# FFN, second attention and experts of a gated cross-attention program in one program block with SBUF placed by hand

## Chip, cores and metric
One core of a Trainium2 chip. The metric is the device time of one execution in microseconds (us); lower is better.

## What is computed
Two gated cross-attention layers over x (32 x 112 x 256) and a context (32 x 375 x 256), 16 heads of 16, each followed by a feed-forward part: first a three-layer one with weights of +1 and -1, then eight experts of which each token uses one.

```python
x = x + tanh(g_xattn[0]) * L0_xattn(layernorm(x), ctx, ctx, mask_ik, ...)
x = x + tanh(g_ffn[0])   * L0_ffn(layernorm(x), k0, k1, k2, s0, s1, s2)     # 256 -> 1024 -> 1024 -> 256
x = x + tanh(g_xattn[1]) * L1_xattn(layernorm(x), ctx, ctx, mask_if, ...)
x = x + tanh(g_ffn[1])   * L1_ffn(layernorm(x), Wr, W1, W2)
# L1_ffn: eidx = argmax(softmax(x @ Wr)); rank of a token in its expert, kept below cap = 448;
#         xe = x[dispatch]; ye = relu(xe @ W1[e]) @ W2[e]; y[dispatch] += ye * probability
```

## The kernel before
Five stages run one after the other: setup, first attention, FFN, second attention, experts. Each is a program block of its own in which the five engines (PE the matrix engine, ACT, DVE, POOL and SP, which issues most transfers) each run a program written out by hand and wait on each other's semaphores. At the end of a block all engines meet, and then a small block follows in which SP clears the stage's semaphores one by one (`Semaphores.clear`, L93 to L98).

**Attention** (`attention_phase`) is a pipeline over the 32 examples of the batch. In step s, context s is split into a high and a low half-precision part, keys of s-1 are made, values and the row maxima of s-3, exponentials and weighting of s-4, output of s-5; in the second attention examples s-6 to s-16 are normalised, routed to experts and their rows sent to the DRAM buffer `expert_in` (L743). The order of the work inside a step is written out for each engine (`body`). Ahead of the steady part, `run_quads` (L487) interleaves nine steps of `Queries` (L287), which load four examples of x (L326), take statistics (L377), normalise them to `xn` (L364), transpose (L431), multiply by the query weights (L422) and store the result split in two to DRAM (L332), with the first steps of the attention, by the lists ORDER (PE, ACT, DVE, POOL) and LOADS (SP), L481 to L484. The DVE program of the second attention begins with memsets of padding (L1198 to L1219). `store_max` (L643) writes the row maxima, turned, into row 96 of `q_stack`; the next score product of PE waits for it. POOL multiplies eight of twelve units of the probabilities by a mask (L724), and in the second attention it carries much of the routing (L729 to L781).

**Blank rows.** `clear_experts` (L676) fills `expert_in` (3612 KB) with rows that belong to nobody, from SP's queue at step 8 of the first attention.

**FFN** (`ffn_phase`) works on groups of four examples. Step s does the sixteen hidden products of group s-1 (z 0 to 15, L1627) and its output (L1638), and beside them normalises group s: statistics at z 9 (L1477), xn at z 11, transposes on PE at z 12, the low part at z 13. `run_steps` (L68) writes out the first four steps and the last one; steps 4 to 7 run in a hardware loop. SP loads x (L1447) and mask_in (L1448) of a group as soon as the output of the group two before is done, and stores the cut mask for the second attention (L1451, L1453). POOL stores the output y (L1466), which the second attention reads. The FFN's weights `ffn_w` are given free after the FFN.

**Experts** (`experts_phase`): per expert SP loads w1 and w2 (L1717, L1718) and the expert's 448 rows (L1720); ACT and DVE split eight pieces of the weights into high (L1802) and low (L1842) halves, beside the products of the expert before; PE transposes the rows (L1758) and multiplies by w1 (L1775) and w2 (L1789); POOL gathers the rows of the output so far (L1738) and scatters the sums (L1743). For the first expert nothing runs beside the splitting. DVE begins with memsets of `x_old` (L1837).

```python
        setup_phase(nc, m, a)
        attention_phase(nc, m, 0, a["x"], x1, ...)
        ffn_phase(nc, m, a, x1, x2, a["mask_BxSxS2_if1"], add_1, keep_1)
        of_ffn.close()
        attention_phase(nc, m, 1, x2, out, ...)
        experts_phase(nc, m, a, expert_in, out)
```

Of the kernel before, what the change touches and what calls it, by code (L numbers as in the profile page):

```python
# [1 line left out]

# [13 lines left out]
P = 128  # L16
# [27 lines left out]
LARGEST = 3.0e38  # L44

# [54 lines left out]

def flamingo_program(nc, a, out):
# [10 lines left out]
    with ExitStack() as ctx:  # L112
        def sb(name, shape, dt):
# [23 lines left out]
        of_ffn = ctx.enter_context(ExitStack())  # L137
        m["ffn_w"] = [of_ffn.enter_context(nc.sbuf_tensor(f"ffn_w{n}", shape, F16))
                      for n, shape in enumerate(((P, KC, F), (P, FC, F), (P, FC, D)))]
        setup_phase(nc, m, a)  # L140
        attention_phase(nc, m, 0, a["x"], x1, a["ctx_1024"], (m["mask_add"], m["keep"]), q_split,
                        a["mask_1x1xSxS2_ik1"], (None, expert_in))
        ffn_phase(nc, m, a, x1, x2, a["mask_BxSxS2_if1"], add_1, keep_1)
        of_ffn.close()
        attention_phase(nc, m, 1, x2, out, a["ctx_1024"], (add_1, keep_1), q_split, None,
                        (a["L1_ffn_Wr"], expert_in))
        experts_phase(nc, m, a, expert_in, out)


# [137 lines left out]
class Queries:  # L287


    def __init__(self, m, layer, x_in, mask, q_split, sb, sem):  # L290
        self.m, self.layer, self.mask = m, layer, mask
# [195 lines left out]
def run_quads(count, lag, eng, order, queries, body):  # L487
# [7 lines left out]
    for s in range(1 + max(s for what, s in order if what == "a"), count + lag):  # L495
        body(Quad(s // 4, s % 4))


def attention_phase(nc, m, layer, x_in, x_out, context, masks, q_split, mask_in, routing):
# [3 lines left out]
    with ExitStack() as ctx:  # L503
        sems = Semaphores(nc, ctx)
        def sb(name, shape, dt):
            return ctx.enter_context(nc.sbuf_tensor(name + tag, shape, dt))

        def sem(name):
            return sems.new(name + tag)

        def many(count, make, name, *args):
            return [make(f"{name}{n}", *args) for n in range(count)]

        SPILL = P - CK
        WIDE = CH * P
        ctx_in = many(2, sb, "ctx_in", [P, KC, S2], F32)
        ctx_high = many(4, sb, "ctx_high", [P, KC * S2 + SPILL], F16)
        ctx_low = many(4, sb, "ctx_low", [P, KC * S2 + SPILL], F16)
        k_high, k_low = many(2, sb, "k_high", [P, KC, WIDE], F16), many(2, sb, "k_low", [P, KC, WIDE], F16)
        k_stack = many(4, sb, "k_stack", [P, NP * WIDE], F16)  # L520
        q_stack = many(4, sb, "q_stack", [P, NP * 2 * S + P - S], F16)
        values = many(2, sb, "values", [CK, CH, H, QUAD], F32)
        masked_scores = sb("masked_scores", [S, 3, S2], BF16)
        row_max = sb("row_max", [S, H], F32)
        max_parts = sb("max_parts", [S, 2, P], F16)
        max_t = many(2, sb, "max_t", [H // 2, S], F16)
        probs = sb("probs", [CK, UNITS, GT], F32)
        heads_t = sb("heads_t", [P, GT], F32)
        inverse = sb("inverse", [S, H], F32)
        heads_q = sb("heads_q", [S, H, DK], F32)  # L530
        if layer:
            heads_n = sb("heads_n", [P, KC, S], F32)
        else:
            heads_high, heads_low = sb("heads_high", [P, KC, S], F16), sb("heads_low", [P, KC, S], F16)
            wo_high, wo_low = sb("wo_high", [P, KC, D], F16), sb("wo_low", [P, KC, D], F16)
        x_sum = many(4, sb, "x_sum", [S, D], F32)
        router, expert_in = routing
        if layer:
            wr = sb("wr", [P, KC, E], F32)
            stats, mean_var = sb("stats", [S, 6], F32), sb("mean_var", [S, 2], F32)  # L540
            root, shift, half, spread = (sb(n, [S, 1], F32) for n in ("root", "shift", "half", "spread"))
            sent_rows = sb("sent_rows", [S, 3 * G, ROW], F32)
            xt = many(2, sb, "xt", [P, KC, S], F32)
            before_f, before = sb("before_f", [S, S], F32), sb("before", [S, S], BF16)
            ones = sb("ones", [S, S], BF16)
            number, logits = sb("number", [S, G, E], F32), many(2, sb, "logits", [S, G, E], F32)
            shifted, hit, marked, power = (sb(n, [S, G, E], F32) for n in ("shifted", "hit", "marked", "power"))
            chosen, ranks, picked = sb("chosen", [S, G, E], BF16), sb("ranks", [S, G, E], F32), sb("picked", [S, G, E], F32)
            counted, carried = sb("counted", [S, E], F32), sb("carried", [S, E], BF16)
            top, first, chance, rank, over, place = (sb(n, [S, G], F32) for n in  # L550
                                                     ("top", "first", "chance", "rank", "over", "place"))
            put = many(3, sb, "put", [S, G], U32)
            mask_add = many(4, sb, "mask_add", [S, S2 + SPILL], BF16)
            keep = many(4, sb, "keep", [CK, CH, S], I32)
        else:
            mask_add, keep = [masks[0]] * 4, [masks[1]] * 4

        ctx_loaded, q_loaded, k_loaded = many(2, sem, "ctx_loaded"), many(2, sem, "q_loaded"), many(2, sem, "k_loaded")
        max_loaded = [many(2, sem, f"max_loaded_{half}_") for half in range(2)]
        masks_loaded = many(4, sem, "masks_loaded")  # L560
        x_loaded, x_stored = many(4, sem, "x_loaded"), many(4, sem, "x_stored")
        if layer:
            wr_loaded, measured, rooted, xn_ready = sem("wr_loaded"), sem("measured"), sem("rooted"), sem("xn_ready")
            routes_made, routes_kept, powered = sem("routes_made"), sem("routes_kept"), sem("powered")
            reduced, combined = sem("reduced"), sem("combined")
            before_made, numbered, sent = sem("before_made"), sem("numbered"), many(3 * G, sem, "sent")
        queries = Queries(m, layer, x_in, mask_in, q_split, sb, sem)
        pads_set, ones_set = sem("pads_set"), sem("ones_set")
        ctx_high_ready, ctx_low_ready = sem("ctx_high_ready"), sem("ctx_low_ready")
        k_made, k_high_ready, k_low_ready = sem("k_made"), sem("k_high_ready"), sem("k_low_ready")  # L570
        v_made, v_ready = sem("v_made"), sem("v_ready")
        rows_scored, rows_maxed = sem("rows_scored"), sem("rows_maxed")
        parts_ready, max_turned, max_ready = sem("parts_ready"), sem("max_turned"), sem("max_ready")
        scored, exped, masked, weighted = sem("scored"), sem("exped"), sem("masked"), sem("weighted")
        heads_ready, heads_turned, inverted, normed = (sem("heads_ready"), sem("heads_turned"), sem("inverted"),
                                                       sem("normed"))
        turned_back, back_high_ready, back_ready = sem("turned_back"), sem("back_high_ready"), sem("back_ready")
        wo_split = sem("wo_split")
        projected, summed = sem("projected"), sem("summed")
        ended = ExitStack()  # L580
        block = ended.enter_context(nc.Block())

        row_bank = m["bank"][0:3]
        score_bank = m["bank"][3:6]
        head_bank = m["bank"][6]
        work_bank = m["bank"][7]
        HALF = UNITS // 2
        HH = H // 2
# [17 lines left out]
        def bank_of(n, what):  # L606

            return row_bank[use_of[n.value, what] % 3]
# [1316 lines left out]
```

## Time and profile before

| | us |
|---|---|
| median of 3 runs | 1663.68 (1658.14 to 1667.85) |
| the profiled execution, its own time | 1670.54 |
| its span | 1668.9 |
| PE busy | 1486.5 (89%) |
| DVE, POOL, ACT busy | 1067.6, 853.8, 818.5 |
| mean granted TensorE clock | 0.955 of full speed |
| first PE work of the second attention / last PE work of the FFN | 902.27 / 883.57 |
| first PE work of the experts / last of the second attention | 1489.22 / 1455.44 |

The page divides the span into forty slices; in those at the start of a stage PE's share drops to 4 or less of ten, in all others of the two attentions and the FFN it is 8 or 9. A matrix product's end is modelled, so that "busy" at PE only says that nothing was waited for. "x8" at the end of a row of the timeline means that eight like instructions are merged, and the bracket is the idle time of the engine ahead of the row and what ended it.

### The profile page before, as it was taken

Reading aid. Unit: us, or ns where it says so; the run is one execution under the profiler, and the core shown is the slowest. Engines: PE = TensorE matmul, PEld = TensorE weight load, DVE = VectorE, ACT = ScalarE, POOL = GpSimd, SP = SyncE. Lnnn points to the kernel's source line nnn. Section 1 sums busy time; section 2 is a strip of 40 time slices with the busy share of each in tenths; the row PEclk is TensorE's granted clock in tenths of the full one; section 3 lists DMA queues with packets and bytes.
Section 4 is the critical chain, followed back from the end, with each engine's and each line's share of the span. In section 5 each row is a group of like instructions: output and inputs, shape, how many; then the busy total and the mean of one; then the engine's idle time right before and its main releaser. Section 6 shows DMA issues by size and latency. Waiting matters only on the chain. (4 is left out here: it accounts for less than half of the span.)

```text
span 1668.9 us, 41243 instructions
## 1 busy us (share of the span) xinstructions
PE 1486.5 (89%) x15435; PEld 1082.2 (65%) x15435; DVE 1067.6 (64%) x3580; ACT 818.5 (49%) x1907; POOL 853.8 (51%) x904
## 2 busy tenths in 40 slices
PE   0889899999999499999994789999999999529997
PEld 0457678777777266666663457777777777417776
DVE  5767677777777255555545677777777777226663
ACT  3456566666666222222221456666667666314442
POOL 0077677777777000000000177778888888723442
PEclk9999899999999699999997999999999999759999
DMA  5755544544441222222214866655566553063440
GB/s 147 197 130 147 124 102 104 101 102 102 101 93 39 61 63 63 63 71 63 62 36 117 203 125 115 116 113 110 113 128 122 121 108 57 21 187 101 155 137 19
DMA packets 214248, 172.67 MB, mean 103 GB/s; under 512 B 69930, under 2 KB 207599, under 8 KB 214056
## 3 DMA queue, kind: packets, MB, share of 16 engines
q1 hardware_dynamic: 208424, 160.34, 41.8%
q0 software_dynamic: 5632, 9.78, 1.9%
q8 instruction: 119, 1.95, 0.5%
q14 instruction: 73, 0.60, 0.1%
HBM read 95.86 MB, written 41.15 MB: 82 GB/s over the span
## 5 line engine op out<-in xcount | busy, mean ns | idle before, releaser
L1100 ACT ACTIVATE probs_a<-bank 125x448 f32<-125x448 f32 x768 | 384.7, 540 | 23.7 <-PE bank L944 15.0
L724 POOL TENSOR_TENSOR probs_a<-probs_a,mask_keep 125x448 int32<-125x448 int32 x256 | 285.5, 1138 | 108.2 <-ACT probs_a L1100 108.1
L1272 DVE CUSTOM_DVE_ANT_0 masked_scores_a<-bank,mask_add_a 112x375 bf16<-112x375 f32 x512 | 262.5, 547 | 106.0 <-PE bank L914 105.5
L724 POOL TENSOR_TENSOR probs_a<-probs_a,keep_a 125x448 int32<-125x448 int32 x256 | 286.1, 1137 | 66.4 <-ACT probs_a L1100 65.0
L1272 DVE CUSTOM_DVE_ANT_0 masked_scores_a<-bank,mask_add 112x375 bf16<-112x375 f32 x512 | 261.1, 550 | 85.5 <-PE bank L914 82.0
L914 PE MATMUL bank<-k_stack_a,q_stack_a 96*128 96x375 f16 x1024 | 292.4, 326 | 5.8 <-DVE row_max_a L1272 4.6
L944 PE MATMUL bank<-q_stack_a,k_stack_a 97*128 97x224 f16 x1536 | 254.6, 261 | 11.7 <-DMA q_stack_a<-max_t_a 10.7
L944 PEld LDWEIGHTS bank<-q_stack_a,k_stack_a 97*128 97x128 f16 x1536 | 147.0, 99 | 72.7 <-DMA q_stack_a<-max_t_a 12.3
L789 POOL TENSOR_TENSOR ctx_low_a<-ctx_in_a,ctx_high_a 128x375 f16<-128x375 f32 x128 | 113.1, 904 | 146.2 <-ACT ctx_high_a L1078 146.1
L1627 PE MATMUL bank<-h0h_f,ffn_w 128*128 128x448 f16 x512 | 180.5, 352 | 0.0
L1627 PE MATMUL bank<-h0l_f,ffn_w 128*128 128x448 f16 x512 | 180.4, 352 | 0.0
L1466 POOL DMA_DIRECT2D x_after_ffn<-y_f x8 | 5.9, 741 | 333.7 <-DVE y_f L1513 333.7
L962 PE MATMUL bank<-probs_a,values_a 125*32 125x112 f32 x6144 | 161.5, 260 | 1.9 <-POOL probs_a L724 1.9
L962 PEld LDWEIGHTS bank<-probs_a,values_a 125*32 125x32 f32 x6144 | 144.8, 110 | 22.6 <-issue 19.5
L1153 ACT ACTIVATE heads_t_a<-bank 128x448 f32<-128x448 f32 x64 | 34.8, 544 | 216.7 <-PE bank L962 216.7
L914 PEld LDWEIGHTS bank<-k_stack_a,q_stack_a 96*128 96x128 f16 x1024 | 99.5, 98 | 45.2 <-DVE row_max_a L1272 13.7
L1578 ACT ACTIVATE h1h_f<-bank 128x448 f16<-128x448 f32 x64 | 34.8, 544 | 152.9 <-PE bank L1627 152.9
L871 PE MATMUL bank<-wv_high,ctx_high_a 128*128 128x256 f16 x384 | 105.3, 274 | 1.4 <-DVE k_low_a L1315 1.4
L871 PE MATMUL bank<-wv_high,ctx_low_a 128*128 128x256 f16 x384 | 104.9, 273 | 0.0
L871 PE MATMUL bank<-wv_low,ctx_high_a 128*128 128x256 f16 x384 | 104.7, 273 | 0.0
L1506 DVE SCALAR_TENSOR_TENSOR h1l_f<-bank,h1h_f 128x448 f16<-128x448 f32 x64 | 39.8, 621 | 97.3 <-ACT h1h_f L1578 97.3
L850 PE MATMUL bank<-ctx_high_a,wk_high 128*128 128x375 f16 x256 | 84.2, 329 | 6.9 <-DVE k_low_a L1315 6.6
(215 smaller groups left out, 3193.0 us busy)
## 6 DMA issues: line engine op xcount, KB each, us to landing
k_stack_a<-k_high_a SPq DMA_DIRECT2D x256, 96.0 KB, 4.0
ctx_in_a<-in_ctx_dram SPq DMA_DIRECT2D x64, 375.0 KB, 3.6
w_in_e<-in_L_ffn_W_dram SPq DMA_DIRECT2D x16, 1024.0 KB, 8.6
k_stack_a<-k_low_a SPq DMA_DIRECT2D x128, 96.0 KB, 4.5
q_stack_a<-q_split SPq DMA_DIRECT2D x128, 84.0 KB, 3.4
q_split<-high_a SPq DMA_DIRECT2D x32, 224.0 KB, 3.7
mask_in_f<-in_mask_BxSxS_if_dram SPq DMA_DIRECT2D x8, 656.2 KB, 6.4
mask_keep<-keep_f SPq DMA_DIRECT2D x8, 656.2 KB
```

What stands on the lines that cost most here:

```text
L724: pool.tensor_tensor(bits, bits, cols, ALU.mult).then_inc(masked, 1)
L789: pool.tensor_tensor(ctx_low[s.four][:, cols], ctx_in[s.two][:, c, :], ctx_high[s.four][:, cols], ALU.subtract).then_inc(ctx_low_ready, 1)
L850: last = pe.matmul(work_bank[:, 0:S2], w[:, c, j * P:(j + 1) * P], part[p.four][:, c * S2:(c + 1) * S2], start=c == 0 and n == 0, stop=c = ...
L871: last = pe.matmul(work_bank[:, (k % 2) * D:(k % 2 + 1) * D], part[x.four][:, at:at + P], w[:, c, :], start=c == 0 and n == 0, stop=c == K ...
L914: pe.matmul(bank_of(x, h)[:, 0:S2], q_stack[x.four][0:STACK, at:at + P], k_stack[x.four][0:STACK, (h // 2) * WIDE:(h // 2) * WIDE + S2], s ...
L944: last = pe.matmul(bank[:, half * 2 * S:(half + 1) * 2 * S], k_stack[d.four][0:ROWS, at:at + P], q_stack[d.four][0:ROWS, (2 * t + half) * ...
L962: last = pe.matmul(head_bank[QUAD * j:QUAD * (j + 1), t * S:(t + 1) * S], values[d.two][:, k, 4 * t + j, :], probs[:, i, j * S:(j + 1) * S ...
L1100: act.activation(probs[:, i, :], score_bank[i % 3][0:CK, 0:GT], ACT.Exp, scale=DK ** -0.5).then_inc(exped, 1)
L1153: act.activation(heads_t[:, :], head_bank[:, 0:GT], ACT.Copy).then_inc(heads_ready, 1)
L1272: dve.tensor_tensor_reduce(masked_scores[:, use_of[x.value, h] % 3, :], bank_of(x, h)[0:S, 0:S2], mask_add[x.four][:, 0:S2], 1.0, -LARGEST ...
L1506: dve.scalar_tensor_tensor(out=low[:, j, :], in0=z_bank[z % 4][:, 0:GT], scalar=0.0, in1=high[:, j, :], op0=ALU.max, op1=ALU.subtract).the ...
L1627: last = pe.matmul(z_bank[z % 4][:, 0:GT], w[layer][:, c, j * P:(j + 1) * P], part[:, c, :], start=c == 0 and n == 0, stop=c == chunks - 1 ...
```

## The change
FFN, second attention and experts become programs that are run one after the other in one block (`run_block`); there is no meeting of the engines and no clearing of semaphores between them, and all their semaphores are cleared after the experts. Buffers of the three are placed by hand in regions (`Region`), so that the second attention's context, key and query buffers lie outside the FFN's and the first expert's weights and rows outside what the attention still uses. In the last FFN step each engine does the first items of the second attention's ORDER and LOADS (q 0, q 1, a 0). The FFN's steps are all written out. `clear_experts` moves from step 8 of the first attention to step 2 of the FFN. The first expert's weights are loaded in eight pieces in steps 20 to 27 of the second attention and split in steps 28 to 31. The FFN uses the PSUM banks in another order. Where the block end ordered things, there are waits now.

```diff
-        attention_phase(nc, m, 0, ...); ffn_phase(...); of_ffn.close(); attention_phase(nc, m, 1, ...); experts_phase(...)
+        with ExitStack() as first:
+            run_block(nc, attention_phase(m, place, place, sems.new, 0, a["x"], x1, ...))
+            sems.clear()
+        with ExitStack() as second:
+            of_ffn = Region(nc, start, FFN_SIZE)
+            of_start = Region(nc, start + FFN_SIZE, EARLY_SIZE)
+            after = Region(nc, base, start + FFN_SIZE - base)
+            early = Region(nc, start + FFN_SIZE, CTX_SIZE)
+            asked = Region(nc, start + FFN_SIZE + CTX_SIZE, EARLY_SIZE - CTX_SIZE)
+            spare = Region(nc, start + FFN_SIZE + EARLY_SIZE, SPARE_SIZE)
+            last = Region(nc, base, start + FFN_SIZE - base)
...
+            of_the_ffn = Program(*(partial(part, after=attention) for part in ffn[0:5]))
+            run_block(nc, of_the_ffn, attention, experts)
+            sems.clear()

 class Queries:                                       # sync, tensor
+            if self.layer:
+                sp.wait_ge(self.ffn.stored[s % 2], 16 * (s // 2 + 1))
             sp.dma_start(self.xg[s % 2][:, :, :], self.x_rows[s]).then_inc(self.x_loaded[s % 2], 16)
...
+            if self.layer and q == 0:
+                pe.wait_ge(self.ffn.y_ready, G * NG)
...
+            if self.layer and p == 0:
+                pe.wait_ge(self.ffn.kept, 2 * NG)

 def attention_phase(...):
+    def load_beside(sp, s):
+        if layer and 20 <= s < 28:
+            experts.load_first(sp, s - 20)
+    def high_beside(act, s):
+        if layer and 28 <= s < 32:
+            experts.high_first(act, 2 * (s - 28))
+            experts.high_first(act, 2 * (s - 28) + 1)
+    def low_beside(dve, s):
+        if layer and 28 <= s < 32:
+            experts.low_first(dve, 2 * (s - 28))
+            experts.low_first(dve, 2 * (s - 28) + 1)
...                                                   # SP, layer 1
-                if not layer and s.value == 8:
-                    clear_experts()
+        if opening:
+            load_context(Quad(0, 0))
+            body(Quad(0, 0))
+            return
+            sp.wait_ge(ffn.y_ready, G * NG)
+            for n in range(2):
+                sp.wait_ge(ffn.stored[n], 16 * NG // 2)
             sp.dma_start(wr[:, :, :], ...)
-            run_quads(B, LAG, sp, LOADS, queries.sync, body)
+        run_quads(3, B + LAG, sp, LOADS[done:], queries.sync, body, load_beside)
...                                                   # DVE, layer 1, ahead of the memsets
+            for n in range(2):
+                dve.wait_ge(ffn.stored[n], 16 * NG // 2)
+                dve.wait_ge(ffn.add_stored[n], 16 * NG // 2)
+                dve.wait_ge(ffn.keep_stored[n], 16 * NG // 2)

 def ffn_phase(...):                                  # s == NG is the last step
-    z_bank, y_bank, turn_bank = m["bank"][0:4], m["bank"][4:6], m["bank"][6:8]
+    z_bank, y_bank, turn_bank = m["bank"][2:6], m["bank"][6:8], m["bank"][0:2]
-            run_steps(sp, NG, 1, body)
+        for s in range(NG + 1):
+            if s == NG:
+                after.queries.sync(sp, 0)
+                after.queries.sync(sp, 1)
+                after.sync(sp, opening=True)
+            if s == 2:
+                clear_experts()
+            body(Step(s // 2, s % 2))
+            if s == NG:
+                after.gpsimd(pool, opening=True)
+                if s.value == NG and z == 11:
+                    after.queries.vector(dve, 0)
+                if s.value == NG and z == 13:
+                    after.queries.vector(dve, 1)
+                if s.value == NG and z == 12:
+                    after.queries.scalar(act, 0)
+        after.scalar(act, opening=True)
+        after.queries.scalar(act, 1)
+                    if s.value == NG and b == 1:
+                        after.queries.tensor(pe, 1)

 def experts_phase(...):
+    def load_first(sp, n):
+        rows = piece(w1_rows[0], w2_rows[0], n)
+        sp.dma_start(piece(w1_in[0], w2_in[0], n), rows).then_inc(first_loaded, 16)
+    def high_first(act, n):
+        act.wait_ge(first_loaded, 16 * PIECES)
+        act.activation(piece(w1[0][0], w2[0][0], n), ...).then_inc(w_high_ready, 1)
+    def low_first(dve, n):
+        dve.wait_ge(w_high_ready, n + 1)
+        dve.scalar_tensor_tensor(out=piece(w1[1][0], w2[1][0], n), ...).then_inc(w_low_ready, 1)
+                if s.value > 0:
                     sp.dma_start(w1_in[s.slot][:, :, :], ...)
                     sp.dma_start(w2_in[s.slot][:, :, :], ...)
+                else:
+                    for n in range(3 * G):
+                        sp.wait_ge(sent[n], 16 * len(range(n, B, 3 * G)))
                     sp.dma_start(xg[s.slot][:, :, :], ...)
```

## Rows read from the trace of the kernel before

**Rows 1.** Windows, one steady step of the second attention: busy time by engine, clock, DMA.
```profile
1324.70:1339.25 14.55, 14.55 (x191) 11.34 (x190) 10.78 (x44) 9.89 (x25) 13.11 (x16) 1.00 0.62 119
```

**Rows 2.** Chain of waits, its start: start us, us, what.
```profile
1487.82 4.90 DVE w_low_e L1842 x8
...
1493.93 11.61 PE bank L1775 x48
```

**Rows 3.** Timelines by engine, seam from FFN to second attention: start us, us, instruction.
```profile
885.02 0.71 POOL L1466 DMA_DIRECT2D x_after_ffn<-y_f  x1 [37.10 <-DVE y_f L1513]
...
891.81 0.16 DVE L1198 MEMSET max_parts_a<- 112x120 uint32 x1 [7.45 <-PEq L94]
...
896.08 0.16 DVE L1219 MEMSET number_a<- 112x4 f32 x8
...
900.84 1.38 DVE L364 TENSOR_SCALAR xn_a<-xg_a,mean_var_q_a,scale_a 112x256 f32<-112x256 f32 x4
...
902.27 1.76 PE L431 MATMUL bank<-ident,xn_a 112*128 112x112 f32 x8 [18.43 <-DVE xn_a L364]
...
909.54 0.93 PE L431 MATMUL bank<-ident,xn_a 112*128 112x112 f32 x8
...
914.89 0.98 PE L431 MATMUL bank<-ident,xn_a 112*128 112x112 f32 x8 [0.40 <-DVE xn_a L364]
```

**Rows 4.** Timelines of SP and PE, first expert's rows; landing times of all eight such loads.
```profile
1478.36 0.57 SPq L1720 DMA_DIRECT2D xg_e<-expert_in  x1
...
1489.22 1.75 PE L1758 MATMUL bank<-ident,xg_e 112*128 112x112 f32 x8 [33.52 <-DMA xg_e<-expert_in]
...
DMA to landing us min/median/max: 2.0/2.5/16.4
```

**Rows 5.** ACT's heads in three steps of the first attention, PE's wait, the clear's landing.
```profile
160.37 0.54 ACT L1153 ACTIVATE heads_t_a<-bank 128x448 f32<-128x448 f32 x1 [3.28 <-PE bank L962]
...
183.78 0.54 ACT L1153 ACTIVATE heads_t_a<-bank 128x448 f32<-128x448 f32 x1 [3.28 <-PE bank L962]
...
197.40 0.54 ACT L1153 ACTIVATE heads_t_a<-bank 128x448 f32<-128x448 f32 x1 [3.28 <-PE bank L962]
...
172.89 0.93 PE L944 MATMUL bank<-q_stack_a,k_stack_a 97*128 97x224 f16 x4 [7.24 <-DMA q_stack_a<-max_t_a]
...
DMA to landing us min/median/max: 14.3/14.3/14.3
```

**Rows 6.** Timelines of SP, DVE and POOL inside the FFN.
```profile
608.09 0.29 SPq L1453 DMA_DIRECT2D mask_keep<-keep_f  x1
...
628.06 1.40 DVE L1477 BATCH_NORM_STATS2 stats_f<-xg_f 112x6 f32<-112x256 f32 x4
...
691.55 0.71 POOL L1466 DMA_DIRECT2D x_after_ffn<-y_f  x1 [37.94 <-DVE y_f L1513]
730.61 0.71 POOL L1466 DMA_DIRECT2D x_after_ffn<-y_f  x1 [38.35 <-DVE y_f L1513]
```

**Rows 7.** Instructions by source line: last waits seen, semaphore clears (ns, first and last start).
```profile
L1470 POOLq EVENT_SEMAPHORE  x1: 17/17/17, 888.7 to 888.7; - x1
...
L98 SPq EVENT_SEMAPHORE_RANGE_CLEAR  x28: 25/28/30, 889.9 to 891.4; - x28
...
L1381 POOLq COMPARE_BRANCH  x1: 45/45/45, 1468.0 to 1468.0; - x1
...
L98 SPq EVENT_SEMAPHORE_RANGE_CLEAR  x91: 25/30/49, 1471.4 to 1477.1; - x91
```

**Rows 8.** Timelines of SP, ACT and DVE between two steps of the second attention.
```profile
1249.17 0.33 SPq L704 DMA_DIRECT2D out_dram<-x_sum_a  x1
1252.37 0.68 SPq L643 DMA_DIRECT2D q_stack_a<-max_t_a  x1
...
1339.25 0.55 ACT L1153 ACTIVATE heads_t_a<-bank 128x448 f32<-128x448 f32 x1 [3.49 <-PE bank L962]
...
1339.73 0.55 DVE L1272 CUSTOM_DVE_ANT_0 masked_scores_a<-bank,mask_add_a 112x375 bf16<-112x375 f32 x1 [1.36 <-PE bank L914]
```

More of the change, by code:

```diff
@@ L1 @@
+import math
+from collections import namedtuple
 from contextlib import ExitStack
+from functools import partial
 import concourse.bass as bass
@@ L143, in flamingo_program, with place @@
[L143 to L147, printed above, removed]
+        with ExitStack() as first:
+            sems = Semaphores(nc, first)
+            def place(name, shape, dt):
+                return first.enter_context(nc.sbuf_tensor(name, shape, dt))
+            run_block(nc, attention_phase(m, place, place, sems.new, 0, a["x"], x1, a["ctx_1024"],
+                                          (m["mask_add"], m["keep"]), q_split, a["mask_1x1xSxS2_ik1"]))
+            sems.clear()
@@ new lines, in flamingo_program @@
+        with ExitStack() as second:
+            sems = Semaphores(nc, second)
+            start = -(-nc.sbuf_base // 32) * 32
+            of_ffn = Region(nc, start, FFN_SIZE)
[5 more added lines that the diff above has]
+            last = Region(nc, base, start + FFN_SIZE - base)
+            ffn = ffn_phase(m, of_ffn, sems.new, a, x1, x2, a["mask_BxSxS2_if1"], add_1, keep_1, expert_in)
+            sent = [sems.new(f"sent{n}") for n in range(3 * G)]
+            experts = experts_phase(m, last, early, asked, spare, sems.new, a, expert_in, out, sent)
+            attention = attention_phase(m, after, of_start, sems.new, 1, x2, out, a["ctx_1024"], (add_1, keep_1), q_split,
+                                        None, (a["L1_ffn_Wr"], expert_in, sent), ffn, experts)
+            of_the_ffn = Program(*(partial(part, after=attention) for part in ffn[0:5]))
+            run_block(nc, of_the_ffn, attention, experts)
+            sems.clear()
@@ L484, with run_quads @@
          ("a", 2), ("q", 9), ("q", 10))
-def run_quads(count, lag, eng, order, queries, body):
+def run_quads(first, count, eng, order, queries, body, beside=None):
     for what, s in order:
@@ new lines, in turn_maxima, with score_unit @@
+        def turn_maxima(n, half):
+            pe.wait_ge(parts_ready, 2 * n.value + half + 1)
+            wait_bank(pe, n, HALVES[half])
+            dst = bank_of(n, HALVES[half])[:, :].bitcast(F16)[:, 0:S]
+            pe.transpose(dst, max_parts[:, half, :], ident_h[0:S, 0:S]).then_inc(max_turned, 1)
+        def score_unit(d, i):
+            t, k = divmod(i, CH)
+            if i % HALF == 0:
+                pe.wait_ge(max_loaded[i // HALF][d.two], 16 * (d.use2 + 1))
+            if i == 0 and layer:
+                pe.wait_ge(masks_loaded[d.four], 32 * (d.use4 + 1))
+            if i == 0 and isinstance(d.value, int) and d.value == 0:
+                pe.wait_ge(ones_set, 6)
+                pe.wait_ge(queries.low_ready, KC * NG)
+            wait(pe, exped, UNITS * d.value + i - 2)
+            bank = score_bank[i % 3]
+            by_scores = i not in pool_units
+            if by_scores:
+                pe.matmul(bank[:, 0:GT], mask_add[d.four][:, k * CK:k * CK + P],
+                          ident_b[0:S, 0:S].unsqueeze(1).to_broadcast([S, 4, S]), start=True, stop=True)
+            for half in range(2):
+                at = (2 * t + half) * WIDE + k * CK
+                last = pe.matmul(bank[:, half * 2 * S:(half + 1) * 2 * S], k_stack[d.four][0:ROWS, at:at + P],
+                                 q_stack[d.four][0:ROWS, (2 * t + half) * 2 * S:(2 * t + half + 1) * 2 * S],
+                                 start=not by_scores, stop=True, skip_group_check=True)
+            last.then_inc(scored, 1)
```

2327 lines of the change are left out of this document (1163 added, 1164 removed).

## The prediction
> **What bounds the kernel now.** I read the page first: the matrix engine (PE) is busy for 89% of the span, and the slices in which it is not lie at the start of each stage. Then the windows by stretch, for what sets the pace inside a stage: one step of the second attention is 14.55 us and PE is busy for all of it, with POOL at 13.11 and DVE at 10.78 [rows 1]. Then the chain of waits, which runs back from the end over PE alone until it reaches the first expert's first product at 1493.93 and, ahead of that, the splitting of that expert's weights [rows 2]. So inside the stages PE is the limit and a faster helper engine is worth nothing; what can be won lies where PE stands still. The timelines show three such places, and the change touches all three. (1) FFN to second attention: PE waits 18.43 us [rows 3]. (2) Attention to experts: PE waits 33.5 us [rows 4]. (3) Step 8 of the first attention takes 23.41 us, from 160.37 to 183.78, where its neighbour takes 13.62, because PE waits 7.24 us for a small transfer and then runs some time at half clock [rows 5].
>
> **The blank rows (clear_experts).** The 3.6 MB write is issued on SP's queue in step 8 of the first attention and lands after 14.3 us; the transfer of the row maxima that PE waits for is queued behind it [rows 5]. Taken away, the step should be like its neighbour: 23.41 - 13.62 = 9.8 us gained. In the FFN it is issued right behind the keep store of 608.09, so at its old duration it lands near 623. Behind it in the queue lies the load of group 2, which is normalised at 628.06 [rows 6]; that leaves some 5 us for 448 KB. I cost it at nothing. The cover is that the FFN keeps a whole group (38.6 us) of loads ahead; were the cover gone, the price is at most the 9.8 of before. Ends: 0 to -9.8, nearest to 0.
>
> **The FFN without its loop.** Steps 4 to 7 of the FFN ran in a hardware loop. POOL's wait from store to store is 37.94 in an unrolled step and 38.35 in the first looped one [rows 6]; the three other looped ones lie between. With some 0.25 for each of four: 1.0 us gained. Ends: 0 and 1.6.
>
> **First seam.** Before: the last store of the FFN is issued at 885.02 and seen as landed at 888.7 [rows 3, 7]. Then come the end of the block and 28 semaphore clears to 891.4 [rows 7], DVE's memsets from 891.81 to 896.24, loads, statistics, xn of group 0 at 900.84, PE's first transposes at 902.27, the second ones at 909.54, the third at 914.89 [rows 3]. After: loads, statistics, xn and transposes of group 0, and the statistics of group 1, lie inside the last FFN step, in the place where DVE and ACT otherwise prepare a next group that no longer exists, and the two loads and two context loads are issued some 40 us ahead. Only the eight transposes come on PE's path: 0.93 us at full clock [rows 3], so the last store is seen at 889.6. SP and DVE both wait for that store. SP's queue behind this wait holds the router weights and the load of group 2; DVE's holds the memsets and everything after. The memsets take their 4.4 us to 894.0, the reciprocals and xn of group 1 1.8 us (as 0.4 and 1.38 before 902.27 [rows 3]), so the second transposes start near 895.9 instead of 909.54: 13.6 us. In the meantime PE computes the query product of group 0 and then stands still for some 7 us. After the 18 us pause the granted clock was at its lower level, 1.2 GHz (the page's slices), and the eight transposes took 1.76 instead of 0.93 [rows 3]; I expect the lower level here too, so from the second transposes to the third it takes the 7.27 us of the cold pair of before, not the 5.35 of the next: -1.9. That leaves 11.7; I take 11.5. Ends: 3, if the later loads of the prologue, and not this start, set its length, and 13.6.
>
> **Second seam.** Before: POOL has seen all rows sent at 1468.0; the block's end and 91 clears follow to 1477.2 [rows 4, 7]; the rows of expert 0 are loaded at 1478.36 behind 2 MB of weights, and PE starts its transposes at 1489.22 [rows 4]; ACT and DVE split eight weight pieces until 1492.7, and the first product starts at 1493.93 [rows 2]. After: the weights are there and split; SP issues the load of the rows as soon as the last row has landed, at about 1468.1. Its landing took 2.0 us at best and 10.9 in this seam [rows 4]; now it is first in its queue with 2 MB right behind it, so I take 4.0: 1472.1. Transposes (1.75 [rows 4]), one copy and one subtraction: 3.4 us, where it was 4.7 with ACT still on the weights. First product at 1475.5 instead of 1493.93: 18.4 us. Ends: 11.5 and 20. The second expert's weights are asked for some 9 us earlier too, and the next pair at once, since the pieces of expert 0 count as done; both lie in the queue behind what PE waits for first.
>
> **What is given back.** The clears do not vanish, they gather behind the last store: 28 of the FFN and 91 of the attention [rows 7], 1.5 + 5.7 = 7.2 us, on the path that sets the end. Ends: 6.6 and 7.8.
>
> **What the attention takes in.** Steps 20 to 27 each issue one 256 KB piece on SP, between the store at 1249.17 and the maxima of 1252.37, a gap of 3.2 us [rows 8]; at the clear's rate (3.6 MB in 14.3 us) a piece is 1.0 us, so it fits. Steps 28 to 31 each put two pieces on ACT and DVE ahead of the body. ACT stands idle there for 3.49 us, DVE for 1.36 [rows 8]; two low pieces on DVE are 2 x 0.61 = 1.2 us (4.90 for eight [rows 2]). It just fits on DVE, and what is late next is the row maximum and the bank behind it. I take -1.0 in all. Ends: 0 and -12 (the first rival).
>
> **Sum.** 9.8 + 1.0 + 11.5 + 18.4 - 7.2 - 1.0 = 32.5 us. The profiled execution took 1670.54, so one like it would take 1638.0; it was 6.9 us over the median, and against the median of 1663.68 the forecast is 1631 us.
>
> **Rivals.** (A) The attention pays for what it takes in. Each low piece reads two SBUF tiles on DVE while POOL, 13.11 of 14.55 us busy in 16 instructions [rows 1], masks the probabilities; if each piece waited for one POOL instruction of 0.82 us, that is 6.6 us, and 2 MB of loads at the clear's price (9.8 us for 3.6 MB) are 5.4. Against it: the seam between two steps, where the pieces lie, is the one place where POOL has only small work. 12 instead of 1.0 lost: 1642. The Trainium skill, "SBUF — State Buffer", section "SBUF: two separate sides", has the rule: DVE instructions with two SBUF inputs and GpSimd instructions that read SBUF share one port pair, and the loser blocks for the whole instruction. By that rule the 6.6 us would stand and the sum would be 5.6 us smaller; in the trace of before DVE split weights only while POOL computed nothing, so no row there decides it. (B) The prologue's gain is not kept, because its loads and the traffic through the split queries set its length: 3 instead of 11.5, 1640. For it: the queue of SP is long there. Against it: each later load waits on xn, which comes earlier. (C) The clear keeps its price in the FFN: group 2 is late, DVE waits in order, PE's transposes after it: 1641. Against it: the 5 us of room. (D) Slower: the new placing makes the second attention's own step longer. PE has no slack there, POOL 1.4 us. The gain of 32.5 is eaten at 1.0 us in each of 32 steps, and from 1.3 us on the kernel is slower than before, 1672 or more. For POOL's eight masks that would be (1.4 + 1.3) / 8 = 0.34 us each on 0.82. Nothing in the rows points to it. (E) The change does not do what it says: the waits that stand in for the two block ends come as late as these, both seams give nothing, the clears still come on top, and 9.8 + 1.0 - 7.2 - 1.0 = 2.6 are left: 1661.
>
> **How the numbers follow.** Forecast 0.68, A 0.11, B 0.09, C 0.07, D 0.03, E 0.02. Half a per cent, 8.3 us, is about what a measurement of this kernel can tell from no change. Forecast, A, B and C lie below 1655 and make faster 0.95; E is same, 0.02; D slower, 0.03. The range: the unknown ends of the forecast's terms reach from 38 (13.6 at the first seam, 20 at the second, no loss in the attention) to some 22 gained, and A to C lie at 1640 to 1642; with the runs' own spread of 5 us, 1622 to 1643.
>
> **What would show it.** Right: step 8 of the first attention 13.6 long; FFN steps of 38.6 with PE full; the second transposes of attention 1 some 11 us after the last store is issued and the clock low again for some 10 us; steps 20 to 31 at 14.55 to 14.81; the first product of expert 0 some 7 us after the last row is seen landed; 139 or more clears at the end, over 8 us. Wrong: a step of 28 to 31 above 15, PE idle in FFN step 2 behind a transpose, or a wait for the first rows of over 6 us.

## The result and the profile after

The changed kernel takes 1650.72 us, the median of 8 executions (1646.99 to 1659.43); the kernel before takes 1665.75 in its 8 beside them. The ratio of the two is 0.9919 (95% interval 0.9897 to 0.9942): faster beyond the interval, but by less than one per cent, 15.0 us where 32.5 were forecast. 1650.7 lies outside the range of 1622 to 1643. The profiled execution took 1659.43 (span 1657.2); it is the longest of the eight, as will matter below.

Where the gains were forecast they are there. Timelines of the changed kernel, the first attention and the first seam:

```profile
156.95 0.54 ACT L1255 ACTIVATE heads_t_a<-bank 128x448 f32<-128x448 f32 x1 [3.28 <-PE bank L1065]
170.58 0.54 ACT L1255 ACTIVATE heads_t_a<-bank 128x448 f32<-128x448 f32 x1 [3.28 <-PE bank L1065]
...
875.39 0.71 POOL L1582 DMA_DIRECT2D x_after_ffn<-y_f  x1 [6.05 <-DVE y_f L1631]
885.64 1.75 PE L512 MATMUL bank<-ident,xn_a 112*128 112x112 f32 x8 [7.46 <-DVE xn_a L439]
893.62 0.93 PE L512 MATMUL bank<-ident,xn_a 112*128 112x112 f32 x8
902.62 0.99 PE L512 MATMUL bank<-ident,xn_a 112*128 112x112 f32 x8 [0.38 <-DVE xn_a L439]
```

The step that held the blanking write is 13.63 long (170.58 - 156.95), where it was 23.41 [rows 5]: 9.8 gained. The transposes of group 0 now lie inside the FFN, so these three are the second, third and fourth of the stage. The second come 10.25 after the last FFN store (24.52 before [rows 3]), the third 18.23 (29.87 before). Counted from that store to the first heads copied by ACT (965.48, before 987.16), the seam is 12.05 shorter, where 11.5 was forecast. The forecast had the eight transposes of group 0 in it, and they lie ahead of the store: the last FFN step is 38.72 instead of 37.82, so like for like the seam gained 11.15. The second seam:

```profile
1464.59 0.32 SPq L1875 DMA_DIRECT2D xg_e<-expert_in  x1
...
1468.29 1.75 PE L1911 MATMUL bank<-ident,xg_e 112*128 112x112 f32 x8 [15.82 <-DMA xg_e<-expert_in]
...
1471.43 0.53 PE L1928 MATMUL bank<-x_high_e,w_high_e 128*128 128x448 f16 x1 [1.38 <-DVE x_low_e L2004]
```

The rows landed in 3.66 us and PE waits 15.82, not 33.52 [rows 4]. The first product stands at 1471.43 instead of 1493.93 [rows 2] although the attention before it ended only 0.9 earlier: 21.6 gained, forecast 18.4.

**Where time was lost again: four places.** First, the second attention. Its first heads are 21.68 us earlier than before, its last (1434.85, before 1435.76) only 0.91. A body is one step of an engine's program there; bodies 20 to 27 each issue a load of the first expert's weights, bodies 28 to 31 each split two pieces. Windows of four steps, body 27 to body 30 (us, then the busy time of PE, PEld, DVE, ACT and POOL with instructions, granted clock, DMA share, GB/s):

```profile
1288.74:1304.19 15.45, 14.71 (x191) 11.43 (x191) 11.64 (x46) 11.05 (x27) 13.24 (x13) 1.00 0.60 117
1304.19:1324.84 20.65, 16.37 (x191) 12.32 (x190) 16.84 (x47) 10.96 (x27) 14.31 (x18) 0.92 0.46 84
1324.84:1346.58 21.74, 18.00 (x191) 13.28 (x190) 16.58 (x47) 11.23 (x28) 14.36 (x17) 0.84 0.44 81
1346.58:1361.39 14.81, 14.81 (x196) 11.61 (x195) 11.96 (x49) 11.02 (x28) 12.18 (x12) 1.00 0.64 113
```

Bodies 28, 29 and 31 (20.86) are 6.1 to 7.2 longer than before, 19.6 together; body 30, with the same two pieces, loses nothing. Bodies 25 and 27, among those with a load, lose 1.1 and 0.9. The chain of waits of the changed kernel has three steps that the chain of before has not:

```profile
1310.32 5.07 DVE max_parts_a L1391
...
1330.96 4.53 DVE max_parts_a L1391
1367.50 4.40 DVE max_parts_a L1391
```

These are single instructions of 112 x 8 numbers, with a median of 0.17 us. In the kernel before the longest of them took 1.79 (ns, min/median/max; L1281 there is L1391 here):

```profile
L1281 DVE TENSOR_SCALAR max_parts_a<-row_max_a x128: 160/172/1794, 96.3 to 1423.1; 112x8 f16<-112x8 f32 x128
```

The timelines round the first of the three (DVE and POOL, with the PE instruction that follows):

```profile
1303.19 1.28 DVE L1860 SCALAR_TENSOR_TENSOR w_low_e<-w_in_e,w_high_e 128x512 f16<-128x512 f32 x2
1303.19 1.39 POOL L876 TENSOR_SCALAR over_a<-rank_a 112x4 f32<-112x4 f32 x1
...
1307.11 5.52 POOL L825 TENSOR_TENSOR probs_a<-probs_a,keep_a 125x448 int32<-125x448 int32 x5
...
1310.32 5.07 DVE L1391 TENSOR_SCALAR max_parts_a<-row_max_a 112x8 f16<-112x8 f32 x1
...
1312.57 0.59 POOL L830 TENSOR_TENSOR root_a<-spread_a,half_a 112x1 f32<-112x1 f32 x1
1313.13 2.22 POOL L825 TENSOR_TENSOR probs_a<-probs_a,keep_a 125x448 int32<-125x448 int32 x2
...
1315.90 0.33 PE L1017 MATMUL bank<-k_stack_a,q_stack_a 96*128 96x375 f16 x1 [4.28 <-DVE row_max_a L1382]
```

Read it from the top. The two low pieces do not wait: 1.28 us as planned. POOL's small operation that starts with them takes 1.39 instead of 0.25, so POOL is 1.1 late. POOL then runs eight operations on end from 1307.11 to 1315.35, and DVE's small TENSOR_SCALAR, begun at 1310.32, ends when POOL's row ends. PE needs the next row maximum and stands still for 4.28; the granted clock of the two steps falls to 0.92 and 0.84, which adds to the pause. In body 30 POOL has a gap of 0.67 us from 1352.4 on, and the same instruction, at 1352.69, takes 0.16. The wait was there in small before the change: the 1.79 us instance, at 968.22, ends together with two POOL instructions that follow each other without a gap (968.24 to 969.98), in the start of the stage.

Second, the blanking write in the FFN. Timelines of SP, DVE and POOL, and the write's time to landing:

```profile
594.25 1.00 SPq L1549 DMA_DIRECT2D expert_in<-nobody  x1
599.37 6.25 SPq L1557 DMA_DIRECT2D xg_f<-x_after_attention  x1
...
616.75 1.40 DVE L1595 BATCH_NORM_STATS2 stats_f<-xg_f 112x6 f32<-112x256 f32 x4 [2.75 <-DMA xg_f<-x_after_attention]
...
643.13 0.74 POOL L1582 DMA_DIRECT2D x_after_ffn<-y_f  x1 [42.17 <-DVE y_f L1631]
...
DMA to landing us min/median/max: 21.1/21.1/21.1
```

The write takes 21.1 us here and not 14.3 [rows 5]; the issue of the load behind it takes 6.25 us instead of some 0.3, group 2 is late, and that step is 43.08 instead of 38.60: 4.5 lost. Without the loop the four steps that were looped are 0.8 shorter together (forecast 1.0).

Third and fourth, the end. Its rows by source line (ns, first and last start):

```profile
L112 POOLq DRAIN  x1: 8553/8553/8553, 1639.7 to 1639.7; - x1
...
L103 SPq EVENT_SEMAPHORE_RANGE_CLEAR  x140: 25/30/45, 1648.5 to 1656.9; - x140
```

and the same two of the kernel before:

```profile
L1883 POOLq DRAIN  x1: 5273/5273/5273, 1662.0 to 1662.0; - x1
...
L98 SPq EVENT_SEMAPHORE_RANGE_CLEAR  x20: 25/28/30, 1667.5 to 1668.6; - x20
```

140 clears take 8.4 us, where the last 20 took 1.1 before: 7.3, as forecast. But POOL's drain ahead of them, the instruction with which POOL leaves the block, takes 8.55; before, the last one took 5.27 and another of 2.78 lay in the second seam. The last store is 22.3 earlier, the end 11.7.

### The profile page after: what moved, and what is told of

The parts are those of the page before. It is cut to its first block, busy times and chain, and to the rows that moved or that the text cites. A ratio compares the mean times of both kernels' runs of the same rounds, so it can differ in the third digit from the quotient of the medians.

```text
span 1657.2 us, 40853 instructions
## 1 busy us (share of the span) xinstructions
PE 1485.0 (90%) x15435; PEld 1081.2 (65%) x15435; DVE 1079.0 (65%) x3580; ACT 818.5 (49%) x1907; POOL 854.5 (52%) x904
## 4 chain that ended last, share of the span: by engine, by line
PE 55%; DMA 4%; DVE 3%; POOL 1%; issue 1%; ACT 1%; SPq 1%; POOLq 0%; DVEq 0%; ACTq 0%
PE bank L1754 14%; PE bank L1942 5%; PE bank L1017 5%; PE bank L1928 5%; PE bank L1047 4%; PE bank L1065 4%; PE bank L953 4%; PE bank L974 4%; PE bank L1765 3%; DMA q_stack_a<-max_t_a 1%; PE bank L1097 1%; PE bank L1043 1%; DMA xg_f<-x_after_attention 1%; DVE max_parts_a L1391 1%; PE bank L1073 1%
## 5 line engine op out<-in xcount | busy, mean ns | idle before, releaser
L1017 PE MATMUL bank<-k_stack_a,q_stack_a 96*128 96x375 f16 x1024 | 293.0, 326 | 17.4 <-DVE row_max_a L1382 16.2
```

Source lines behind the costliest of these rows:

```text
L1017: pe.matmul(bank_of(x, h)[:, 0:S2], q_stack[x.four][0:STACK, at:at + P], k_stack[x.four][0:STACK, (h // 2) * WIDE:(h // 2) * WIDE + S2], s ...
```

## The experiments

Theory 1: the stalls come from a port into SBUF, the engines' on-chip memory, that DVE and POOL share. The two-input pieces hold POOL up, POOL loses the gaps between its masks, and then the TENSOR_SCALAR waits until POOL runs out of work. Theory 2: DVE's 1.3 us in the step is the cost. Theory 3: ACT's high pieces or the loads. The expectations call bodies 28, 29 and 31 steps 24, 25 and 27: they count a step by the heads that it ends with. The changed kernel is the base of each edit, 1650.72; each ratio is to the kernel before, run beside it.

**Low pieces at the end of DVE's work** (e1_low_late).

```diff
     def low_beside(dve, s):
-            experts.low_first(dve, 2 * (s - 28))
-            experts.low_first(dve, 2 * (s - 28) + 1)
...
     def vector(dve):                                  # experts_phase
+        for n in range(PIECES):
+            low_first(dve, n)
```

> The eight low pieces move from steps 28 to 31 of the second attention to the end of DVE's work there, just ahead of the two blanking memsets. The high pieces on ACT and the loads stay. Theory 1 (the two-input pieces on DVE hold POOL's small operation up by 1.1 us, and the 112x8 TENSOR_SCALAR then waits out POOL's row of masks): steps 24, 25 and 27 go from 20.7-21.7 back to 14.6-14.9, some 19 us less in the attention; the pieces lie where PE waits anyway, so the time is 1650.7 - 19 = about 1632 (1628 to 1640). Theory 2 (DVE's own 1.3 us in the step is the cost): the same here. Theory 3 (the high pieces on ACT make the delay, or the loads): the steps stay at 20 or more, at most 3 us gained, 1648.

Measured: 1641.85 (1640.81 to 1642.89), ratio 0.9862 (0.9836 to 0.9888). Bodies 28 to 31 take 14.55 to 14.88, so theory 3 falls. The gain in the median is 9 and not 19, and the time is outside the 1628 to 1640 expected: the profiled execution of the changed kernel had three stalls and was the longest, the others took 1646.99 to 1655.37. The changed kernel's times spread over 12.4 us and this one's over 2.1, which fits a number of stalls that differs from one execution to the next; no trace of the others shows it.

**The same time on DVE without the port** (e2_dve_fill), on top of the first.

```diff
+    def fill(dve, n):                                 # called in steps 28 to 31
...
+        dve.memset(w1[1][0][:, :, :].bitcast(F32), 0.0).then_inc(filled, 1)
+        dve.memset(w2[1][0][:, 0:2, :].bitcast(F32), 0.0).then_inc(filled, 1)
```

> As the kernel with the low pieces at the end, but DVE gets two memsets of 0.91 and some 0.4 us in their old place in steps 28 to 31: the same time on DVE, no input read from SBUF. Theory 1: POOL's small operation stays at 0.25 to 0.3 us, the steps stay below 15.2, time within 4 us of the kernel with the pieces at the end. Theory 2 (DVE's time alone): three or four of the steps take 20 us again, 12 to 20 us more than with the pieces at the end.

Measured: 1639.94 (1638.38 to 1641.50), bodies 28 to 31 at most 14.97. A routing operation of POOL that overlaps the memset keeps its 0.31 us (beside the pieces it took 1.39, at 1323.90 in the changed kernel); timelines of DVE and of POOL:

```profile
1314.05 0.91 DVE L1866 MEMSET w_low_e<- 128x1024 f32 x1 [0.15 <-issue]
...
1313.95 0.31 POOL L853 TENSOR_SCALAR hit_a<-shifted_a 112x32 f32<-112x32 f32 x1
```

Theory 2 falls, with the limit that the memsets together take 1.2 us and the pieces 1.3.

**POOL late, nothing on DVE** (e3_pool_late; the second with the memset twice, e8_pool_two), both with the low pieces at the end. The memset stands at the end of POOL's body, so it bears on the step behind.

```diff
+            if layer and 28 <= s.value < 32:          # gpsimd, ahead of the routing operations
+                experts.fill(pool, s.value - 28)      # memset, 128 x 1024 f32; e8: two of them
```

> As the kernel with the low pieces at the end, but POOL gets one memset of some 1.0 us ahead of its small routing operations in steps 28 to 31, and DVE nothing. Theory 1 (POOL 1.1 us late has no gap between its masks, and the 112x8 TENSOR_SCALAR of DVE waits 4 to 5 us until the row ends): three of the four steps take 20 to 22 us, TENSOR_SCALAR L1391-like instructions of 4 to 5 us are there, 15 to 20 us more than with the pieces at the end. Theory 2 (DVE's time): steps at most 1 us longer each, 0 to 4 us in all.

> Low pieces at the end; POOL gets two memsets, 2 us together, ahead of its small operations in steps 28 to 31 (one memset gave one step of 21.4 and 2.9 us in the median). Theory 1: POOL has still less of a gap, so two to four of the steps take 20 to 23 us, each with one TENSOR_SCALAR of 4 to 5 us: 1650 to 1665. Rival (the one long step was chance, not POOL's lateness): none or one, 1642 to 1648.

Measured: with one memset (0.94 us) 1644.73 (1643.59 to 1646.41) and one stall of 4.76 in the profiled execution, in a step of 21.36; I had expected three such steps. With two, 1660.40 (1658.94 to 1665.36) and three. The chain of waits of the second kernel, and two of its steps:

```profile
1325.18 5.00 DVE max_parts_a L1393
1361.85 5.10 DVE max_parts_a L1393
1382.57 5.76 DVE max_parts_a L1393
```

```profile
1355.70:1376.41 20.71, 16.40 (x191) 12.36 (x191) 16.40 (x44) 9.89 (x25) 14.73 (x19) 0.92 0.36 65
1376.41:1398.98 22.57, 17.60 (x191) 13.04 (x191) 16.46 (x44) 9.50 (x24) 13.89 (x19) 0.85 0.36 61
```

No piece is near these steps: POOL's lateness alone makes the stall, and more of it makes more. The waits end with POOL's row here too: the last, at 1388.33, where POOL's eight instructions from 1380.08 on end at 1388.30.

**Which instruction form waits** (e7_stride on the changed kernel, e9_pool_two_stride on the one with two memsets; then another form, e11_reduce and e10_pool_two_reduce on the same two).

```diff
-    row_max = sb("row_max", [S, H], F32)              # e7, e9: maxima two apart
+    row_max = sb("row_max", [S, 2 * H], F32)
...
-            dve.tensor_scalar(max_parts[:, half, 0:HH], row_max[:, cols], -1.0, None, ALU.mult)
+            dve.tensor_reduce(max_parts[:, half, 0:HH], row_max[:, cols].unsqueeze(2), AX.X, ALU.max,
+                              negate=True)            # e10, e11, on the packed row_max
```

> The changed kernel, pieces in steps 28 to 31 as they are; the row maxima lie two apart in SBUF, so that the 112x8 TENSOR_SCALAR reads every other float. Theory 1a (it is this instruction's fast form over both ports, with contiguous operands, that needs the port which POOL holds): no instance of over 1 us in the second attention, steps 24, 25 and 27 at 14.6 to 15.0, time 1641 to 1643 as with the low pieces at the end. Theory 1b (any SBUF to SBUF TENSOR_SCALAR waits): instances of 4 to 5 us and steps of 20 to 22 remain, time near 1650.

> The same two memsets on POOL, with the row maxima two apart. Theory 1a: no TENSOR_SCALAR of over 1 us; POOL is only 2 us later in a step where it has 1.4 us of slack, so 0 to 1 us a step, 1642 to 1647. Theory 1b: as the kernel with the two memsets alone, within 3 us.

> Two memsets on POOL in steps 28 to 31, low pieces at the end (1660.4 with three stalls of 5 to 6 us, and 1660.2 with the strided input), and the 112x8 TENSOR_SCALAR replaced by a TENSOR_REDUCE over an axis of one element that negates: the same numbers, another form of instruction. The Trainium skill, page SBUF - State Buffer, section Who interferes with whom, says that tensor_scalar can enter a mode over both ports and contends with GpSimd, and that tensor_reduce never does on this chip. If that is the mechanism: no instance over 1 us, steps of 28 to 31 at most 15.6, 1641 to 1647. If it is the reading of row maxima as such, or DVE's order of work, that waits: instances of 5 us again, 1656 to 1662.

> The changed kernel with its pieces in steps 28 to 31, and only the form of this one instruction replaced by the TENSOR_REDUCE. Mechanism right: the pieces then cost next to nothing where they are, steps 24 to 27 at 14.6 to 15.1, and the time is that of the kernel with the pieces at the end, 1641.9 (1639 to 1644). Mechanism wrong: 1648 to 1652 with one to three steps over 20 us.

Measured: the stride changes nothing (1648.49, 1646.85 to 1659.27, one instance of 4.83 and one of 1.69 on the chain; with the two memsets 1660.23, 1656.61 to 1662.79, three of 5.0 to 5.8). The form changes all: with the two memsets 1640.63 (1640.03 to 1640.74), with the pieces in their place 1641.41 (1640.83 to 1643.98), ratio 0.9856 (0.9839 to 0.9872). Source row of the second attention in the kernel with two memsets and the TENSOR_REDUCE, and two of its steps in the region of the memsets:

```profile
L1393 DVE TENSOR_REDUCE max_parts_a<-row_max_a x64: 149/156/163, 938.2 to 1400.7; 112x8 f16<-112x8 f32 x64
```

```profile
1330.51:1345.33 14.82, 14.82 (x196) 11.61 (x195) 10.90 (x46) 11.01 (x29) 14.22 (x16) 1.00 0.63 117
1345.33:1359.88 14.55, 14.55 (x191) 11.34 (x190) 10.72 (x44) 9.88 (x26) 14.11 (x19) 1.00 0.55 93
```

All 64 instances take 0.15 to 0.16, and POOL, busy for 14.22 of 14.82 us, costs PE nothing. So one instruction form carried the whole loss of these steps. The Trainium skill, "SBUF — State Buffer", section "Who interferes with whom", says that tensor_scalar can enter a mode over both ports and then contends with GpSimd, and that tensor_reduce never does on this chip; the waits of the one (up to 5.78 us) and the 0.15 to 0.16 us of all instances of the other agree, though no row names the mode itself. It also says that whoever issues first holds the ports for its whole instruction while the other is blocked; here the loser waited through some five instructions of POOL (5.07 us), as long as these followed one another without a gap, and the measurement decides.

**The other three losses** (e4_ends, with the attention as it was).

```diff
-            if s == 2: clear_experts()                # ahead of the loads of group 2
+            if s.value == 2: clear_experts()          # behind them
...
+            pool.drain()                              # gpsimd, behind the attention's last wait
+                if p.value in (3, 6): pool.drain()    # experts, gpsimd
...
+                if s.value == 2:                      # experts, sync
+                    for old in cleared: sp.sem_clear(old)     # those of FFN and attention
```

> The changed kernel with its attention as it is, and three edits elsewhere: the blanking write is issued behind the loads of group 2 instead of ahead of them; POOL drains once behind the attention's last send and twice between experts; SP clears the semaphores of the FFN and the attention (about 119) during expert 2 instead of at the end. Expected: FFN step 2 from 43.1 to 38.7, -4.5; POOL's last drain from 8.6 to 2 to 3 us, if its length goes with the indirect transfers since the drain before (8 to 9 if it does not): -5.5; some 20 clears left at the end, 1.1 instead of 8.4: -7.2. Together 17 us less than the changed kernel, 1633.5 (1630 to 1640). Rival: the drain placed ahead of the first gather delays PE by up to 3 us, and the final drain keeps its length: -9 in all, 1642.

Measured: 1633.72 (1630.37 to 1636.66), 17.0 less, with two stalls of 5.03 and 4.39 still in the profiled execution. The FFN step is 38.63. Source rows of the drains and the clears of this kernel:

```profile
L939 POOLq DRAIN  x1: 3328/3328/3328, 1457.7 to 1457.7; - x1
...
L1905 POOLq DRAIN  x2: 6569/7062/7555, 1536.9 to 1597.7; - x2
...
L112 POOLq DRAIN  x1: 700/700/700, 1631.8 to 1631.8; - x1
...
L1884 SPq EVENT_SEMAPHORE_RANGE_CLEAR  x107: 25/30/45, 1490.9 to 1497.4; - x107
...
L103 SPq EVENT_SEMAPHORE_RANGE_CLEAR  x33: 25/25/30, 1632.8 to 1634.6; - x33
```

The first drain lies in the time in which POOL waits for the rows, and PE's wait in the seam stays at 15.78 (15.82 in the changed kernel); the rival of the expectation is out. The three edits were run together, not apart. By the rows they are worth 4.5, 7.9 (8.55 - 0.70) and 6.6 (8.4 - 1.8), 19.0 in sum, 2 more than the medians show.

**Everything together** (e5_all: e1 and e4), and then the loads and the high pieces late as well (e12_all_late), and the TENSOR_REDUCE on top of that (e13_all_late_reduce).

```diff
-        if layer and 20 <= s < 28: experts.load_first(sp, s - 20)      # e12, e13
+        if layer and 36 <= s < 44: experts.load_first(sp, s - 36)
...
+        for n in range(PIECES):                       # experts, scalar, ahead of its own work
+            high_first(act, n)
```

> The changed kernel with the low pieces at the end of DVE's attention work, the blanking write behind the loads of group 2, POOL's three earlier drains, and the clears of the FFN's and the attention's semaphores during expert 2. If the parts add up: the kernel with the low pieces at the end stands at 1641.9, and the three other edits took 17 us from the changed kernel (1650.7 to 1633.7), so 1641.9 - 17 = 1625 (1622 to 1629). If the low pieces' stalls had only moved into other waits: 1633 again.

> The kernel with all edits (1624.1), and the loads of the first expert issued in steps 36 to 43 instead of 20 to 27, the high pieces after ACT's attention work. The long steps 21 and 23 or 21 alone (15.5 to 16.2 instead of 14.6) should go: -1.0 to -1.7, so 1622.8 (1621 to 1624.5). Rival: the loads or the splits end behind the last row (they have some 25 us from their issue), and the first product of the experts waits: 1626 to 1632.

> As the kernel before it, with the TENSOR_REDUCE too. With the pieces gone from the steps, single waits of up to 1.8 us of the TENSOR_SCALAR are what is left in both attentions; most lie in slack. -0 to -3 against the kernel without it, 1621 (1619 to 1624).

Measured: e5_all 1624.10 (1623.67 to 1625.62), ratio 0.9755 (0.9739 to 0.9772): 26.6 us less than the changed kernel, the parts add up. e12_all_late 1627.52 (1624.69 to 1628.43), ratio 0.9764 (0.9747 to 0.9780); e13_all_late_reduce 1624.71 (1623.23 to 1626.08), ratio 0.9753 (0.9737 to 0.9769). The last two lie above the ranges expected (1621 to 1624.5, 1619 to 1624). The rival's mechanism, splits that end too late, is not what e12_all_late shows: its low pieces end at 1437.7, and the first rows land at 1451.5. By their ratios these three can't be told apart, so the 1.0 to 1.7 expected of the loads stays open. The version to keep is e5_all. The TENSOR_REDUCE was not run on it; with the pieces late it has little left to win, but it takes away the stall's cause and not one occasion of it.

## Why the prediction was wrong

Against a time of the kind profiled (1670.54 before, 1638.0 forecast, 1659.43 measured), the terms in order:

- **Clear out of the first attention:** 9.8, right. **FFN loop:** 1.0, measured 0.8. **First seam:** 11.5, measured 11.15 (12.05 less the 0.90 of the last FFN step), with 7.98 from the second transposes to the third, at the lower clock (0.58 of full speed granted from 883 to 895), where 7.27 was taken.
- **Second seam:** 18.4, measured 21.6. 2.3 of the 3.2 more lie between the attention's last heads and the issue of its last send (29.55 before, 27.22 now), which the forecast held fixed; the rest in the landing (3.66 for 4.0) and the steps behind it. The 4.0 was right on a misread row: the landing times in [rows 4] are those of all transfers that touch the rows' buffer, gathers and scatters too, and its 2.0 is none of the eight loads. Those alone, by their source line in the kernel before:

```profile
DMA to landing us min/median/max: 3.7/4.2/16.4
```

- **What the attention takes in:** 1.0 forecast, 20.8 measured in that execution; in the medians the stalls alone cost 9 to 11 (0.9919 against 0.9862 and 0.9856 of the two kernels without stalls: 0.57% and 0.63%). This is the step that failed. The prediction asked whether the pieces fit into DVE's idle 1.36 us, and they do; it named POOL's slack of 1.4 us only under rival D. What the pieces take away is POOL's gaps, and what is late next is not the row maximum's own computation but the TENSOR_SCALAR behind it that needs such a gap. "It just fits on DVE" was the wrong test.
- **Rival A** had the price (12) and the port, and the wrong victim: it let the pieces wait for POOL, 0.82 each, and argued that the place between two steps is safe because POOL has only small work there. The small work waited for the pieces, and the bill came 7 us later. That its 12 lies near the 9 to 11 is luck. The rule was weighed only for instructions that the change adds; it holds for those already there too: TENSOR_SCALAR L1281 was there, and its longest instance of 1.79 us was a row of before that could have been read. The 0.82, too, is the mean of all sixteen POOL instructions of a step; a mask takes 1.14.
- **Clear in the FFN:** 0 forecast, 4.5 lost. The step "at its old duration it lands near 623" failed. It was issued where the forecast put it, right behind the keep store (593.93, the program being 14.2 earlier by then), but took 21.1 us for 14.3 and held up the issue of the load behind it, which landed 17.4 us after its issue, and DVE waited 2.75 for it. Rival C had this mechanism at 9.8.
- **The end:** 7.2 for the clears, measured 7.3. The drain was left out: the second seam's gain contains the 2.78 us of a drain which, like the clears, does not vanish. The last drain grew by 3.3, a term that the forecast left at nothing without a reason.

Of 32.5 forecast, then, 9 to 11 went to the stalls, 4.5 to the blanking write, 3.3 to the drain and 0.2 to the loop; 2.8 came back at the seams. That explains 14 to 16 of the 17.5 missing; some 1 to 3 I can't place. The start of the profiled execution of before was 3.4 longer than that of after in code that is the same, and such differences stand between one execution and the median.

The range failed with the sum: it took the rivals one at a time, and here the losses of A's kind and of C's kind and an unlisted one came together.

## What to carry to other kernels

Before filling an engine's idle time, ask what its neighbour on the same port loses: here the neighbour had 1.4 us of slack in 14.55, and a 0.17 us instruction that needed one of its gaps stopped the matrix engine for over 4 us. Where such an instruction can be written in a form that doesn't wait (here a reduction over one element), that takes the cause away; in time it won here as much as moving the pieces did (1641.4 and 1641.9). When two blocks are joined, what stood between them (semaphore clears, drains) is moved to the end and not removed; put each piece of it where its engine waits anyway.

## What the runs showed of the hardware

- The wait of the TENSOR_SCALAR is not bounded by one instruction of POOL: 5.07 us here and up to 5.78 with the two memsets, through some five on end, and it ends within 0.1 us of the end of POOL's gapless row in each of the three of the changed kernel. The number of such waits is not fixed by the attention's code: three in the profiled execution of the changed kernel, two in that of e4_ends, whose attention is the same.
- The other way round, two SCALAR_TENSOR_TENSOR of DVE (1.28 us together) made POOL's hit_a instruction take 1.39 us (at 1323.90); beside a memset of 0.91 us on DVE it took 0.31.
- POOL's drain grew with the number of indirect transfers since the drain before it: 0.70 us for 8, 2.78 and 3.33 for 32, 5.27 for 64, 8.55 for 96, about 0.09 each. That it is their number and nothing else is not shown: the two in the middle of the experts took 6.6 and 7.6, behind gathers just issued. They cost nothing there: from the first product to the last store it is 165.2 us with them and 166.0 without.
- The same 3.6 MB write took 14.3 us to land in the first attention, 21.1 in the FFN, and 17.8 there behind the loads (e4_ends); with the load behind it, the issue of that load took 6.25 us instead of 0.3.
- Taken out of the end, 107 clears took 6.5 us on SP during an expert; by the 165.2 us above, the experts were no longer for it.
